# Perceiver megakernel: a tile of its own for the fourth panel of query weights, and the first 18 groups of maxima read by halves

## The reference

```
q = (layernorm(x) @ Wq).reshape(1, 256, 32, 32)      # 32 query heads of width 32
k = (ctx @ Wk).reshape(1, 4096, 8, 32)               # 8 key/value heads, 4 query heads each
v = (ctx @ Wv).reshape(1, 4096, 8, 32)
scores = q @ k.T * 32 ** -0.5
x = x + (softmax(scores) @ v) @ Wo
```

## Time and profile before

| | us |
|---|---|
| timed runs, median of 3 | 2112.91 (2109.82 to 2115.65) |
| profiled execution, its own time | 2105.75 |
| its span, first to last instruction | 2104.4 |
| PE busy | 1920.4 (91%) |
| DVE busy | 1287.9 (61%) |
| ACT busy | 859.5 (41%) |
| POOL busy | 547.6 (26%) |
| mean granted clock of PE | 0.963 of 2.4 GHz |

### The profile page before, as it was taken

One profiled execution on the slowest core, in us unless ns is written; L12 is line 12 of the kernel. 1 busy time (PEld: TensorE's weight loads), 2 busy tenths in 40 slices (PEclk: granted clock), 3 DMA queues, 4 the chain that ended last, 5 costly groups with the idle time before them and its releaser, 6 DMA issues.

```text
span 2104.4 us, 29620 instructions
## 1 busy us (share of the span) xinstructions
PE 1920.4 (91%) x11932; PEld 1411.2 (67%) x11932; DVE 1287.9 (61%) x1590; ACT 859.5 (41%) x1409; POOL 547.6 (26%) x264
## 2 busy tenths in 40 slices
PE   7899999999997999999998995779999999978977
PEld 5799999999996877787776874423333333366843
DVE  3445444454544787889965855667777775266465
ACT  2211111111113666666663451046777777535421
POOL 0000000000001555554510001036777777510000
PEclk9999999999998999999999998879999999999889
DMA  4533434343326666565724516523433420135052
GB/s 173 173 105 106 125 95 117 98 123 89 88 76 177 203 201 195 189 210 189 237 73 152 188 43 160 125 80 78 96 81 81 94 61 1 38 117 224 1 189 74
DMA packets 154808, 259.30 MB, mean 123 GB/s; under 512 B 36477, under 2 KB 102321, under 8 KB 147505
## 3 DMA queue, kind: packets, MB, share of 16 engines
q1 hardware_dynamic: 154673, 257.42, 40.6%
HBM read 192.39 MB, written 61.76 MB: 121 GB/s over the span
## 4 chain that ended last, share of the span: by engine, by line
PE 81%; DVE 11%; ACT 3%; issue 3%; DMA 2%; SPq 0%; POOL 0%; ACTq 0%; DVEq 0%
PE psum L468 10%; PE psum L1699 7%; PE psum L1716 5%; PE psum L449 4%; PE psum L451 4%; PE psum L450 4%; PE psum L436 3%; DVE top L1888 3%; PE psum L278 3%; PE psum L279 3%; PE psum L280 3%; PE psum L1732 3%; PE psum L809 3%; PE psum L1680 3%; PE psum L811 3%; PE psum L810 3%
## 5 line engine op out<-in xcount | busy, mean ns | idle before, releaser
L1888 DVE TENSOR_REDUCE top<-psum 128x4 f32<-128x2048 f32 x128 | 293.0, 2289 | 118.5 <-PE psum L1680 118.3
L1958 POOL TENSOR_TENSOR added<-probs_f 128x1024 f32<-128x1024 f32 x126 | 299.0, 2375 | 193.6 <-ACT probs_f L1815 141.8
L1815 ACT ACTIVATE probs_f<-psum 128x512 f32<-128x512 f32 x512 | 278.4, 594 | 139.3 <-PE psum L1699 127.1
L601 DVE TENSOR_REDUCE top<-psum 128x2 f32<-128x512 f32 x272 | 186.4, 691 | 198.3 <-PE psum L436 198.2
L900 DVE TENSOR_TENSOR probs_low<-probs,probs_high 128x1024 fp32r<-128x1024 f32 x136 | 195.1, 1438 | 79.1 <-ACT probs L863 78.9
L862 ACT ACTIVATE probs_high<-psum 128x1024 fp32r<-128x1024 f32 x136 | 139.9, 1029 | 160.0 <-PE psum L811 150.3
L1699 PE MATMUL psum<-q_rows,k_rows 97*128 97x512 f32 x512 | 197.5, 461 | 0.7 <-ACT probs_f L1815 0.5
L1699 PEld LDWEIGHTS psum<-q_rows,k_rows 97*128 97x128 f32 x512 | 80.7, 191 | 171.6 <-ACT probs_f L1815 159.1
L449 PE MATMUL psum<-c_high,w_high 128*128 128x256 f32 (+1 forms) x672 | 191.4, 285 | 3.2 <-issue 3.2
L450 PE MATMUL psum<-c_low,w_high 128*128 128x256 f32 (+1 forms) x672 | 191.3, 285 | 0.0
L451 PE MATMUL psum<-c_high,w_low 128*128 128x256 f32 (+1 forms) x672 | 191.0, 284 | 0.0
(11 more groups left out here) (357 smaller groups left out, 3806.3 us busy)
## 6 DMA issues: line engine op xcount, KB each, us to landing
wf_rows<-in_ffn_w_dram SPq DMA_DIRECT2D x42, 512.0 KB, 4.2
staged<-in_ctxT_dram SPq DMA_DIRECT2D x32, 512.0 KB, 4.7
k_four<-k_high SPq DMA_DIRECT2D x128, 128.0 KB, 3.3
wf_rows<-in_ffn_w_dram SPq DMA_DIRECT2D x8, 1376.0 KB, 7.4
q_dram<-wf_turned SPq DMA_DIRECT2D x42, 256.0 KB, 2.3
gate_up<-q_dram SPq DMA_DIRECT2D x10, 1024.0 KB, 8.1
value_high<-v_high SPq DMA_DIRECT2D x32, 256.0 KB, 3.6
value_low<-v_low SPq DMA_DIRECT2D x32, 256.0 KB, 4.3
```

Source lines behind the costliest of these rows:

```text
L601: dve.tensor_reduce(top0[:, r0:r0 + 2, n], psum[:, bank, :].rearrange("p (i n) -> p i n", i=2), AX_X, ALU.max).then_inc(*b.bank_read.up())
L1815: act.activation(probs[:, n % 6, half * BANK:(half + 1) * BANK], psum[:, half, :], ACT.Exp, scale=scale).then_inc(*f.exped.up())
L1888: dve.tensor_reduce(top1[:, :, t, chunk], psum[:, MAXIMA:MAXIMA + G1, :], AX_X, ALU.max).then_inc(*f.max_read.up())
L1958: pool.tensor_tensor(added[pair % 4][:], probs[:, n % 6, :], probs[:, (n + 1) % 6, :], ALU.add).then_inc(*f.added.up())
```

## The change

The fourth panel of query weights (panel 29) gets a tile `q_panel`, at the place in memory where `oT_low` is laid afterwards, and a semaphore `q_panel_in`. It is issued in the stage before, ahead of panels 27 and 28, without a wait. `arrivals` corrects the count of transfers into buffer 2, which now has one fewer. For the first 18 groups of maxima (`HALVED`), PE signals after two of the four matmuls, and again after four; DVE reads banks 4 and 5 after the first signal and 6 and 7 after the second; PE waits before each two matmuls only for the read of the same two banks of the group before. `halves_of` turns a number of groups into a number of signals.

```diff
+        def arrivals(p):
+            return p // 3 + 1 - (p > WQ1 + 3 and p % 3 == (WQ1 + 3) % 3)
+
         def sp_panel(p):
             source, width, k, _ = plan[p]
+            if p == WQ1 + 3:
+
+                sp.dma_start(q_panel[0:k, 0:width], source).then_inc(*second.q_panel_in.up(16))
+                return
...
-            act.wait_ge(*panels_in[p % 3].at(16 * (p // 3 + 1)))
+            act.wait_ge(*panels_in[p % 3].at(16 * arrivals(p)))
...
+        with ExitStack() as early:
+            q_panel = sb(early, "q_panel", [P, KT // 2 * BANK])
+        oT_low = sb(attn1, "oT_low_f", [P, KV1, T], F32R)
...
+        HALVED = 16 + 2
+
+        def halves_of(quads):
+
+            return quads + min(quads, HALVED)
+
         def sp_load_four(kv, piece):
...
-                sp.wait_ge(*second.max_made.at(16 * (kv - 1) + 4 * (piece + 1)))
+                sp.wait_ge(*second.max_made.at(halves_of(16 * (kv - 1) + 4 * (piece + 1))))
...
                 sp_load_values(0)
+                sp_panel(29)
                 sp_panel(27)
                 sp_panel(28)
...
                     if quads:
-                        pe.wait_ge(*f.max_read.at(quads))
+                        pe.wait_ge(*f.max_read.at(halves_of(quads) - (quads < HALVED)))
                     for g in range(G1):
+                        if g == 2 and quads < HALVED:
+                            done.then_inc(*f.max_made.up())
+                            if quads:
+                                pe.wait_ge(*f.max_read.at(halves_of(quads)))
...
-                    both = [panel[(WQ1 + 2 * n + i) % 3] for i in range(2)]
-                    for i in range(2):
-                        p = WQ1 + 2 * n + i
-                        pe.wait_ge(*panels_in[p % 3].at(16 * (p // 3 + 1)))
+                    both = [panel[(WQ1 + 2 * n) % 3], q_panel if n else panel[(WQ1 + 1) % 3]]
+                    pe.wait_ge(*panels_in[(WQ1 + 2 * n) % 3].at(16 * ((WQ1 + 2 * n) // 3 + 1)))
+                    if n:
+                        pe.wait_ge(*f.q_panel_in.at(16))
+                    else:
+                        pe.wait_ge(*panels_in[(WQ1 + 1) % 3].at(16 * ((WQ1 + 1) // 3 + 1)))
...
-                    dve.wait_ge(*f.max_made.at(quads))
-                    dve.tensor_reduce(top1[:, :, t, chunk], psum[:, MAXIMA:MAXIMA + G1, :], AX_X,
-                                      ALU.max).then_inc(*f.max_read.up())
+                    parts = ((0, 2), (2, 4)) if quads <= HALVED else ((0, 4),)
+                    for first, end in parts:
+                        dve.wait_ge(*f.max_made.at(halves_of(quads) - (end < G1)))
+                        dve.tensor_reduce(top1[:, first:end, t, chunk], psum[:, MAXIMA + first:MAXIMA + end, :], AX_X,
+                                          ALU.max).then_inc(*f.max_read.up())
...
                 sp_load_values(1)
-                sp_panel(29)
                 load_queries(1)
```

More of the change, by code:

```diff
@@ L47 @@
     q_high_set q_low_set max_made max_read neg_set neg_turned t_high_set tops_in scored exped added weighed summed
-    upper_set products_read sums_read inverted normed shifted o_high_set o_split""".split()
+    q_panel_in upper_set products_read sums_read inverted normed shifted o_high_set o_split""".split()
 FFN = """gain_in scales_turned scales_copied scales_sent scales_in chunk_in0 chunk_in1 down_in x_rounded
@@ L1636, in second_stage @@
             oT_high = sb(phase, "oT_high_f", [P, KV1, T], F32R)
-            oT_low = sb(phase, "oT_low_f", [P, KV1, T], F32R)
             unit_tiles["fg"] = [[sb(unit_stack, f"panel_fg{i}{part}", [P, 2 * BANK], F32R, "right") for part in "hl"]
```

## The result

| | before | after |
|---|---|---|
| median of 6 runs each, us | 2111.37 (2103.79 to 2120.87) | 2092.07 (2089.44 to 2100.09) |
| ratio, 95% interval | | 0.9924 [0.9897, 0.9951] |
| profiled execution: span, us | 2104.4 | 2096.8 |

The ratio times the 2112.9 us of the prediction is 16.1 us less (10.4 to 21.8); 17.4 was forecast. The two profiled spans, though, differ by only 7.6 us. The next rows are there to explain that before anything is said about the change.

What follows compares the result with a forecast made beforehand. PE was taken as the bound, at the second context attention's start: 11.9 us from the panel wait, the rest from halved reads, less 0.07 lost, sum 17.4 us; from the 2112.91 us median to 2095.5, range 2090 to 2102.

Steps and rivals of the forecast that it cites:

- Part 1: Panel 29's own tile removes PE's wait on the fourth head of queries, with slow clock and restart: 11.87 us saved.
- The hole: PE's 9.64 us wait from 1333.43 in the second context attention, for panel 29's transfer; claimed to go.
- Rival 2: The hole moves: the extra MB holds panel 27 before the first query matmul; 2101 us, chance 0.05.
- Part 2: Reading the first 18 groups of maxima by halves shortens the alternation of PE and DVE; credited with 5.5 us.
- the step of 2.63 us: Time per group of maxima while query matmuls run between groups, forecast at 2.63 us against 2.92 before.
- Groups 14 and 15: Groups of maxima after the last query matmuls: 5.53 us before, 4.68 forecast, 0.85 saved.
- The turn: Turn of the maxima after group 15, 1376.43 to 1378.48 in the kernel before; claimed unchanged.
- Rival 1: The halves bring nothing, only the 11.9 us of the panel's own tile remains; 2101.0 us, chance 0.11.
- What is late next: Small DMA of the maxima behind panels 31 and 32, before the first scores: hardly any slack, costed at 0.
- the stretch: From DVE's first read of maxima (group 0) to the first score matmul; 63.76 us before, 49.11 after.
- Rival 3: The clock stays up in the tail, bringing first score pairs closer; 4.1 us more saved, 2091.4 us, chance 0.09.
- Rival 4: Slower: the score loop fails to raise the clock from 1.2 GHz; 2120 us at 19 pairs, chance 0.03.

Runs made afterwards that it cites:

- e1: The changed kernel with no groups read by halves, so only panel 29's own tile remains; 0.9944 of the kernel before, stretch 51.62 us.
- e3: The changed kernel with the small transfer of the maxima issued ahead of panels 31 and 32 and the last eight k_four pieces; 0.9900 of the kernel before.
- e10: e3 with all 128 groups of maxima read by halves instead of the first 18; 0.9910 of the kernel before.
- e4: The changed kernel with query matmuls placed between the two halves of a group on PE; 0.9947 of the kernel before, stretch 52.47 us.
- e9: The changed kernel with the second values' load moved behind the small transfer of the maxima; 0.9943 of the kernel before, stretch 49.09 us.
- e2: The changed kernel with panel 29 back in the shared buffer, so only the reads by halves remain; 0.9987 of the kernel before, stretch 61.83 us.
- e5: e3 with extra unread matmuls in PE's idle time from group 14 to the first scores; 0.9904 of the kernel before.
- e6: e3 with POOL's memsets of the ones waiting until after the layer norm; 0.9907 of the kernel before.
- e8: The changed kernel measured once more, nothing altered; 0.9933 of the kernel before, stretch 48.87 us.
- e7: e3 with both the extra unread matmuls of e5 and the later memsets of e6; 0.9889 of the kernel before.

## Why the prediction was right, step by step

**Part 1, 11.87 us.** e1 gives 12.1. The hole is gone, with no hole in its place. Panel 27 was issued at 1300.85, behind 11.21 us in which SP stood in the issue of the new tile, and landed after 7.6 us, at 1308.5; panel 28 landed at 1311.0, with PE asking at 1316.97. In e3, whose first query matmul is as early as 1313.10, panel 27 landed at 1307.0. Rival 2 falls. Its reason ("a full queue holds SP") was true, its consequence wasn't.

**Part 2, the step of 2.63 us.** Measured 5.30 or 5.31 us for two groups, 2.65 each; first read of group 0 to that of group 14 36.81 us (1324.32 to 1361.13), forecast 36.47. Groups 14 and 15: 4.64, forecast 4.68. The turn: 2.04, forecast 2.05. A half read takes 1.22 us as extrapolated, and four of them 4.61 in the tail, a pitch of 1.13. The Trainium skill (VectorE: DVE Perf Modes, The TRN2 errata — SBUF-src ops pay a fixed extra latency per instruction) has many small tiles pay the fixed cost per tile; it says so of operations that read SBUF, and the reads here are of PSUM. The trace agrees that there is a fixed part (0.158 us), and not that a second instruction behind the first adds all of it: two halves end 2.35 us after they begin, against 2.29 for a whole read, and e10 shows the same 0.06. The prediction put the full price at 1.5 us (15.9 instead of 17.4); its own sum with a pitch of 1.22 gives 16.4, with 1.25 it gives 16.0, so the page's rule was worth 1.0 to 1.4 us. Rival 1 falls with the steps, and e4 shows the mechanism it feared, a pair that holds PE as long as four, harmless here since the two pairs are adjacent.

**What is late next, priced at 0.** This is the step that was off. The prediction named the right transfer and the right floor, and had the queue dry 10.8 us after the eighth head of queries, 0.3 us before the scores were due. Measured, PE starts 13.27 us after the issue of panels 31 and 32. Stretches of the changed kernel, columns as above:

```profile
1368.00:1372.00 4.00, 1.58 (x4) 0.57 (x4) 4.00 (x4) 0.03 (x1) 0.00 (x0) 0.50 0.94 212
1372.00:1373.00 1.00, 0.00 (x0) 0.00 (x0) 0.43 (x1) 0.00 (x0) 0.00 (x0) 0.50 0.02 2
```

Against the forecast three things add up. Panels 31 and 32 went out 0.6 us later (35.84 us after DVE's first read, forecast 35.2). The traffic lasted until about 1371.8, 11.6 us instead of 10.8. And from its end to PE's start at 1373.43 it is another 1.7 us. The prediction left that out; the rows show nothing else in it but the landing and the signal of the small transfer. Its own rows had a warning: before the change PE started 12.83 us after that issue (1368.73 to 1381.56) without a wait, so they showed the landing only to be no later than that. The floor cost 2.4 us instead of 0: 17.4 - 2.4 = 15.0, against 14.65 and 14.89 measured in the stretch. The prediction's range for its unknowns (14.3 to 18 us) holds that. I then explained it by a backlog of SP's queue, and e9 refuted that. The prediction's sentence that the query copies and panel 30 would go out earlier was wrong as well: SP stood 9.76 us in one of the copies (1335.00) behind the values, and panel 30 went out at 1353.04.

**Parts are not additive.** The prediction credited 5.5 us to the halves. With part 1 they bring 5.0 (e3 against e1), without it 1.9 (e2), since a transfer tied to the queue, not to PE, ends the hole.

**Rival 3**, the clock staying up in the tail, was priced at 4.1 us, and e5 shows 4.06 net in a profile. That close a match is chance: e5 saves 4.87 behind the scores and pays 0.81 in the stretch for its fillers, its first pairs save 1.80 us each and not 1.28, and profiles of kernels without fillers differ by up to 4.8 us from the scores to the end (718.93 in e6, 723.75 in e1). In the two profiles of the changed kernel the rival didn't come true: the granted clock at the first scores is 0.50 in the changed kernel as in the one before (its stretches, columns as in e5 above: us, busy by engine, granted clock, DMA share, GB/s), and the same in e8:

```profile
1365.00:1375.00 10.00, 4.06 (x12) 1.59 (x12) 5.58 (x6) 2.31 (x4) 0.00 (x0) 0.50 0.69 200
1375.00:1385.00 10.00, 9.80 (x30) 3.24 (x30) 2.29 (x1) 4.67 (x9) 4.71 (x2) 0.50 0.00 0
```

**Rival 4** has no sign: scores to end moved by 0.5 and 0.8 us.

**The signs that the prediction named.** It called the forecast wrong if the first scores came after 1368, and the profile has them at 1373.43. That sign was written in time from the start of the span, and 6.5 us of it had been lost before DVE's first read; counted from that read, the limit is 50.2 us, the forecast 46.3 and the measured 49.11. Two more of its signs came out against it: the small transfer does release the first scores late, and the granted clock was not 1.00 from the first query matmul on.

**The total.** 0.9924 and 0.9933 are 16.1 and 14.2 us, with 15 from the stretch. By their intervals (10 to 22, and 9 to 19 us) neither can tell 15.0 from 17.4; the stretch can.

## What to carry to other kernels

When a wait is taken out, price the transfer that ends the next one from issue to landing, signal included, and not to the moment when the queue looks empty; here the difference was 1.7 of 13.3 us. A sign to judge by should be counted from an event close to the change, since what lies ahead of it moved by up to 8 us between executions. Splitting a read pays where producer and consumer take turns in a closed loop, as in the first 14 groups; in the score loop, where PE is the bound, 110 more splits gave nothing. Two gains in front of and behind a wait that another resource ends don't add up, so run each part alone.

## What the runs showed of the hardware

- Two TENSOR_SCALAR instructions of 2 columns on DVE took 2.70 us each beside a 3.5 us POOL memset on one partition, each until that memset's end, and 0.17 without it (e6); a TENSOR_TENSOR of 2 columns beside it took 0.16. No read of the maxima ran beside a memset, so whether those would be slowed is open.
- Two row tiles of 32 rows held PE for 0.43 us, as four did; going back to them from full matmuls added 0.14 us after four records (e4) and 0.08 after eight (the changed kernel).
- Two panels, eight pieces of `k_four` and the small transfer behind them took 12.4 to 13.3 us from the first issue to PE's start, in the five profiles in which PE waited for them. One transfer issue behind the load of values held SP for 9.76 us, another for 11.21 (the changed kernel).
- The granted clock is the largest source of scatter. The eight low-rank matmuls took 3.70 or 5.4 to 6.3 us, the first twenty query records 4.58 or 6.9 to 7.1, and the first score pairs were 2.9 to 3.1 us apart in four profiles, 4.34 in one (e1) and 4.90 in seven, in kernels that are alike in these places. e8 came to its first query matmul 8.4 us later than the first profile of the same program. The granted clock stayed at 0.50 for 15 us of the score loop in the changed kernel although PE was busy nearly throughout (9.80 of 10 us from 1375), and came back after 6 to 7 us in e9. Whether a kernel can steer this stays open: with the filling work the clock was 1.00 through the first scores in e5 and fell again in e7, and e2, e4 and e9 reached fast pairs without it.
